# Moving GpSimd's work in a fused macaron block: low rows, paced preparation, a choice in three parts, attention's last copies

## The reference

```python
x = x + 0.5 * moe(ln(x))      # n=1  16 experts of 176, top 6, and a shared SwiGLU of 352
x = x + mamba(ln(x))          # n=2  selective scan, 512 channels, 16 states, length 256
x = x + 0.5 * moe(ln(x))      # n=3  the same weights as n=1
x = x + 0.5 * ffn(ln(x))      # n=4  SwiGLU of 1024 with Hadamard transforms
x = x + attention(ln(x))      # n=5  16 heads of 16, ALiBi, causal
x = x + 0.5 * ffn(ln(x))      # n=6  the same weights as n=4

# moe: scores = softmax(x @ gate_w.T); top 6, divided by their sum; out += c_e * (silu(g) * u) @ w2_e.T
# mamba: s = exp(d * A) * s + d * B * u ; y = sum_n(s * C_n) + D * u ; out = (y * silu(gate)) @ Wout.T
# ffn: x = fwht(x * SU_ug); up, gate; x = fwht(silu(gate) * up * SU_dp); down, times Wscale_dp
```

## Time and profile before

| | |
|---|---|
| median of 3 runs | 1979.33 us (1977.91 to 1980.43) |
| the profiled execution | 1978.87 us; its span, first to last instruction, 1976.9 us |
| busy TensorE, VectorE, ScalarE, GpSimd | 92%, 69%, 47%, 29% of the span |
| chain that ended last | TensorE 74%, VectorE 13%, issue 7%, ScalarE 6% |
| granted TensorE clock, mean | 0.978 of full speed |

### The profile page before, as it was taken

One profiled execution on the slowest core, in us unless ns is written; L12 is line 12 of the kernel. 1 busy time (PEld: TensorE's weight loads), 2 busy tenths in 40 slices (PEclk: granted clock), 3 DMA queues, 4 the chain that ended last, 5 costly groups with the idle time before them and its releaser, 6 DMA issues.

```text
span 1976.9 us, 26195 instructions
## 1 busy us (share of the span) xinstructions
PE 1827.5 (92%) x9417; PEld 1391.2 (70%) x9417; DVE 1368.7 (69%) x1867; ACT 935.9 (47%) x1776; POOL 577.7 (29%) x383
## 2 busy tenths in 40 slices
PE   7999899999797996998769999999999999998998
PEld 5788688888343543544327888888888887776887
DVE  6666756577999999989995566565676555666533
ACT  3442323333776766676533333232333338887322
POOL 1000604000487776876750000000000024555000
PEclk9999999999898998999999999999999998999999
DMA  5231244110221221221212132231221305552100
GB/s 189 78 105 62 88 150 118 65 61 25 65 69 57 67 70 52 66 65 63 104 44 84 39 104 80 86 102 65 65 73 52 62 1 130 113 111 64 35 11 22
DMA packets 84186, 146.39 MB, mean 74 GB/s; under 512 B 13848, under 2 KB 23704, under 8 KB 83544
## 3 DMA queue, kind: packets, MB, share of 16 engines
q1 hardware_dynamic: 84056, 144.72, 25.2%
HBM read 130.38 MB, written 14.29 MB: 73 GB/s over the span
## 4 chain that ended last, share of the span: by engine, by line
PE 74%; DVE 13%; issue 7%; ACT 6%; DMA 0%; POOL 0%; DVEq 0%; SPq 0%; ACTq 0%; POOLq 0%
PE psum L161 19%; PE psum L162 19%; PE psum L163 19%; DVE scan_state L1570 6%; PE psum L1390 5%; PE psum L1284 2%; PE psum L1944 1%; PE psum L1311 1%; DVE scan_state L1577 1%; PE psum L1370 1%; ACT psum L1497 1%; PE psum L1923 1%; DVE moe_hidden_lo L850 1%; PE psum L1961 1%; ACT attn_p L2092 1%
## 5 line engine op out<-in xcount | busy, mean ns | idle before, releaser
L1166 POOL TENSOR_TENSOR scan_state<-scan_delta_u,scan_B_rows 128x1024 f32<-128x1024 f32 x127 | 299.7, 2369 | 143.4 <-PE psum L1390 129.6
L161 PE MATMUL psum<-xnT_hi,moe_w_hi 128*128 128x512 f32 x800 | 317.9, 397 | 6.1 <-DVE xnT_lo L465 4.2
L162 PE MATMUL psum<-xnT_lo,moe_w_hi 128*128 128x512 f32 x800 | 315.4, 394 | 0.0
L163 PE MATMUL psum<-xnT_hi,moe_w_lo 128*128 128x512 f32 x800 | 313.0, 391 | 0.0
L1570 DVE TENSOR_TENSOR_SCAN scan_state<-psum,scan_state 128x1024 f32<-128x1024 f32 x128 | 292.2, 2283 | 2.3 <-ACT psum L1497 2.0
L777 ACT ACTIVATE moe_hidden<-psum 128x512 f32<-128x512 f32 x200 | 119.6, 598 | 367.5 <-PE psum L163 367.4
L827 DVE TENSOR_TENSOR moe_gated_up<-moe_gate_rows,psum 128x512 f32<-128x512 f32 x184 | 126.5, 688 | 211.4 <-PE psum L163 123.8
L1390 PE MATMUL psum<-scan_state,ident 128*128 128x512 f32 x512 | 255.8, 624 | 0.0
L161 PE MATMUL psum<-moe_w_hi,moe_hidden_hi 128*128 128x256 f32 x800 | 231.0, 289 | 15.9 <-DVE moe_hidden_lo L850 15.0
L413 POOL TENSOR_SCALAR rstd<-mean_var 128x2 f32<-128x2 f32 x48 | 10.5, 220 | 790.9 <-DVE mean_var L447 790.5
L163 PE MATMUL psum<-moe_w_hi,moe_hidden_lo 128*128 128x256 f32 x800 | 227.0, 284 | 0.0
(11 more groups left out here) (226 smaller groups left out, 3513.7 us busy)
## 6 DMA issues: line engine op xcount, KB each, us to landing
scan_B_rows<-scan_B SPq DMA_DIRECT2D x127, 256.0 KB, 3.1
moe_gate_rows<-gate_table SPq DMA_DIRECT2D x176, 128.0 KB, 2.9
...
```

The source lines that it names most:

```text
L161: e.matmul(out, wH, xH, start=start, stop=False)
L162: e.matmul(out, wH, xL, start=False, stop=False)
L163: return e.matmul(out, wL, xH, start=False, stop=stop)
L1166: e.tensor_tensor(self.st[q % self.NBUF][:], self.dtu[:, 2 * h:2 * h + 2, :], self.Bs[:, q % self.RING, :].unsqueeze(1).broadcast_to([P, 2 ...
```

## The change

1. **Scan's low rows.** `rows_lo` of chunks 1 to 3 goes from VectorE at r = 27 to GpSimd at r = 28, behind `times_u`, with a wait for `times_u` in front of it and a wait for itself behind it. That of chunk 0 stays on VectorE.
2. **Preparation in pieces.** The instructions on 1024 and 2048 elements per partition become pieces of 512, and each pair of pieces (or four scalings, or four taps) waits for one more `s_hL`: `Prep.pool` from step 41 to 50, `Scan.early` from step 60 to 67. SyncE's store of them comes at step 53, not 52.
3. **The choice in three parts and two banks.** In the entry, chunks 1 and 3 use bank 7 and chunks 0 and 2 bank 4, their logits, turns and gates come one step earlier (chunk 0's gates stay), and the choice is spread over three steps instead of two. In n=3 the choice has three parts too, and the gates follow one step later.
4. **Attention's last copies.** In the last two units ScalarE splits weight tile 0 before its copies, VectorE copies before it splits, and weight tile 2 of n=6 waits for the last product with V (`read`) instead of for all of attention's output (`freed`).

```diff
 # Tail.choose: part 0 up to the logits less their maximum, part 1 up to match_replace, part 2 the rest
-        k, n, t = self.k, [2 if part == 1 else 0], 4 * self.n
+        k, t = self.k, 4 * self.n
+        n = [(0, 2, 3 + 2 * t)[part or 0]]
...
+        if part == 1:
+            return
+        e.wait_ge(self.r_v.sem, self.r_v.at(3 + 2 * t, c))
         step(e.tensor_tensor(lg, ex, rest, ALU.subtract))
...
 # Glu
-    LATE = 52
-    PE_SLOTS = {2: 1, 3: 3, 5: 4, 6: 5, 9: 6}
-    ACT_SLOTS = {3: 1, 4: 3, 6: 4, 7: 5, 10: 6}
+    LATE = 53
+    PE_SLOTS = {2: 1, 3: 3, 5: 4, 6: 5, 10: 6}
+    ACT_SLOTS = {3: 1, 4: 3, 6: 4, 7: 5, 11: 6}
...
         if self.handed and n == 2:
-            self.prev.freed(e)
+            self.prev.read(e) if self.led else self.prev.freed(e)
...
 # Entry
-    LOGITS = {3: 0, 7: 1, 11: 2, 15: 3}
-    TURN = {4: 0, 8: 1, 12: 2, 16: 3}
-    GATES = {7: 0, 11: 1, 15: 2, 19: 3}
+    LOGITS = {3: 0, 6: 1, 10: 2, 14: 3}
+    TURN = {4: 0, 7: 1, 11: 2, 15: 3}
+    GATES = {7: 0, 10: 1, 14: 2, 18: 3}
...
+    def bank(self, c):
+        return self.k.psum[:, 7 if c % 2 else 4, :]
...
-            if self.LOGITS[j]:
-                e.wait_ge(t.r_cH.sem, t.r_cH.at(1, self.LOGITS[j] - 1))
-            t.pe(e, self.LOGITS[j], 4)
+            if c == 1:
+                e.wait_ge(t.s_xL.sem, t.s_xL.at(2, NCH - 1))
+            elif c:
+                e.wait_ge(t.r_cH.sem, t.r_cH.at(1, c - 2))
+            t.logits(e, c, self.bank(c))
...
 # Scan.early (PACE = 60)
-        e.tensor_copy(self.wH[:], self.raw[:]).then_inc(self.s_wh.sem, 1)
+        w, step = self.raw.shape[1] // 4, self.PACE
+        for n in range(4):
+            if n % 2 == 0:
+                e.wait_ge(self.prev.s_hL.sem, self.prev.s_hL.at(step + 1))
+                step += 1
+            e.tensor_copy(self.wH[:, n * w:(n + 1) * w], self.raw[:, n * w:(n + 1) * w]).then_inc(self.s_wh.sem, 1)
...
 # Scan.pool
+            if r == 28 and c + 1 < NCH:
+                e.wait_ge(self.s_dtu.sem, self.s_dtu.at(2 * c + 3))
+                self.rows_lo(e, c + 1)
+                e.wait_ge(self.s_bc.sem, self.s_bc.at(c + 2))
...
 # Scan.vector
-            if r == 27 and c + 1 < NCH:
-                rows_lo(c + 1)
...
 # Attention.scalar
+            if n == self.N - 2:
+                self.next.early_hi(e, 0)
+                keep(n, 0)
+                keep(n, 1)
             if n and n % 2 == 0:
                 out_hi(n // 2 - 1)
             job(c, u, 1)
-            keep(n, 0)
-            keep(n, 1)
-            if n + 2 >= self.N:
-                self.next.early_hi(e, n + 2 - self.N)
+            if n != self.N - 2:
+                keep(n, 0)
+                keep(n, 1)
+        self.next.early_hi(e, 1)
...
 # Prep.pool (PACE = 41), one of its three butterfly passes
-            e.tensor_tensor(b[:, :, 0, :], a[:, :, 0, :], a[:, :, 1, :], ALU.add).then_inc(self.s_d.sem, 1)
-            e.tensor_tensor(b[:, :, 1, :], a[:, :, 0, :], a[:, :, 1, :], ALU.subtract).then_inc(self.s_d.sem, 1)
+            for to, op in enumerate((ALU.add, ALU.subtract)):
+                e.wait_ge(self.moe.s_hL.sem, self.moe.s_hL.at(step + 1))
+                step += 1
+                for x in range(2):
+                    rows, cols = (slice(x * n, (x + 1) * n), slice(0, f)) if h < 4 else (slice(0, 1), slice(x * f, (x + 1) * f))
+                    e.tensor_tensor(b[:, rows, to, cols], a[:, rows, 0, cols], a[:, rows, 1, cols],
+                                    op).then_inc(self.s_d.sem, 1)
```

More of the change, by code:

```diff
@@ L363, in step @@
                 e.wait_ge(self.r_v.sem, self.r_v.at(n[0], c))
-        if part != 1:
+        if part in (None, 0):
             over = red.unsqueeze(2).broadcast_to([P, t, NEXP])
@@ L372, in choose @@
             return
-        e.wait_ge(self.r_v.sem, self.r_v.at(2, c))
-        e.wait_ge(self.r_ex.sem, self.r_ex.at(1, c))
-        for j in range(t):
-            if j == 0:
-                k.own(e)
-            step(e.max(mx[:, j, :], ex[:, j, :]), wait=(j == t - 1))
-        step(e.memset(mx[:, :, TOPK:8], -1.0))
-        for j in range(t):
-            if j == 0:
-                k.own(e)
-            step(e.match_replace(rest[:, j, :], mx[:, j, :], ex[:, j, :], 0.0), wait=(j == t - 1))
+        if part in (None, 1):
+            e.wait_ge(self.r_v.sem, self.r_v.at(2, c))
+            e.wait_ge(self.r_ex.sem, self.r_ex.at(1, c))
+            for j in range(t):
+                if j == 0:
+                    k.own(e)
+                step(e.max(mx[:, j, :], ex[:, j, :]), wait=(j == t - 1))
+            step(e.memset(mx[:, :, TOPK:8], -1.0))
+            for j in range(t):
+                if j == 0:
+                    k.own(e)
+                step(e.match_replace(rest[:, j, :], mx[:, j, :], ex[:, j, :], 0.0), wait=(part is None and j == t - 1))
+        if part == 1:
+            return
+        e.wait_ge(self.r_v.sem, self.r_v.at(3 + 2 * t, c))
         step(e.tensor_tensor(lg, ex, rest, ALU.subtract))
@@ L857, in vector @@
                 tail.low(e, tc, 1)
-            if tt in (7, 8) and self.guest:
+            if tt in (7, 8, 9) and self.guest:
                 tail.choose(e, tc, tail.bank(), tt - 7)
@@ L969, in dve_late @@
             t.stats(e, (j + 4) // 2, j % 2)
-        if j in self.TURN:
-            t.choose(e, self.TURN[j], self.k.psum[:, 4, :], 0)
-        if j - 1 in self.TURN:
-            t.choose(e, self.TURN[j - 1], self.k.psum[:, 4, :], 1)
+        for part in range(3):
+            if j - part in self.TURN:
+                c = self.TURN[j - part]
+                t.choose(e, c, self.bank(c), part)
         if j in self.BLOCKS:
@@ L1072 @@
     LOADS = 13
+    PACE = 60
     def u(self, c, i):
@@ L1141, in early @@
         e.wait_ge(self.s_load.sem, 16 * self.LOADS)
-        e.tensor_copy(self.wH[:], self.raw[:]).then_inc(self.s_wh.sem, 1)
-        e.wait_ge(self.s_wh.sem, self.s_wh.at(1))
-        e.tensor_tensor(self.wL[:], self.raw[:], self.wH[:].bitcast(F32), ALU.subtract).then_inc(self.s_wl.sem, 1)
+        w, step = self.raw.shape[1] // 4, self.PACE
[4 more added lines that the diff above has]
+            e.tensor_copy(self.wH[:, n * w:(n + 1) * w], self.raw[:, n * w:(n + 1) * w]).then_inc(self.s_wh.sem, 1)
+        e.wait_ge(self.s_wh.sem, self.s_wh.at(4))
+        for n in range(4):
+            if n % 2 == 0:
+                e.wait_ge(self.prev.s_hL.sem, self.prev.s_hL.at(step + 1))
+                step += 1
+            e.tensor_tensor(self.wL[:, n * w:(n + 1) * w], self.raw[:, n * w:(n + 1) * w],
+                            self.wH[:, n * w:(n + 1) * w].bitcast(F32), ALU.subtract).then_inc(self.s_wl.sem, 1)
         e.memset(self.mean[0][:], 1.0 / RANK).then_inc(self.s_one.sem, 1)
@@ L1221, in times_u, with rows_lo @@
         e.tensor_tensor(self.dtu[:, m, :], self.delta[:, m, :], self.pair(c, h), ALU.mult).then_inc(self.s_dtu.sem, 1)
+    def rows_lo(self, e, c):
+        e.wait_ge(self.s_bH.sem, self.s_bH.at(c + 1))
+        e.tensor_tensor(self.bc[32:32 + 2 * NST, c % 2, :], self.wt[1][:], self.bc[0:2 * NST, c % 2, :].bitcast(F32),
+                        ALU.subtract).then_inc(self.s_bc.sem, 1)
     def first_steps(self, e):
@@ L1546, in vector @@
         k, ps = self.k, self.k.psum
-        def rows_lo(c):
-            e.wait_ge(self.s_bH.sem, self.s_bH.at(c + 1))
-            e.tensor_tensor(self.bc[32:32 + 2 * NST, c % 2, :], self.wt[1][:], self.bc[0:2 * NST, c % 2, :].bitcast(F32),
-                            ALU.subtract).then_inc(self.s_bc.sem, 1)
         def convolve(i):
@@ L1614, in vector @@
         e.tensor_copy(self.bc[0:2 * NST, 0, :], self.wt[1][:]).then_inc(self.s_bH.sem, 1)
-        rows_lo(0)
+        self.rows_lo(e, 0)
         tail.both(e, NCH - 1, 1)
@@ L1739, in weight, with read @@
         return self.wH[:, at:at + HID], self.wL[:, at:at + HID]
+    def read(self, e):
+        e.wait_ge(self.s_pv.sem, self.s_pv.at(self.N))
     def freed(self, e):
@@ L2206, in vector @@
             job(c, u, 1)
-            if n + 2 >= self.N:
-                self.next.early_lo(e, n + 2 - self.N)
-        keep(self.N - 1)
+            if n == self.N - 2:
+                self.next.early_lo(e, 0)
+        self.next.early_lo(e, 1)
         out_lo(self.N // 2 - 1)
@@ L2234, in __init__ @@
         arena = Arena(k, "prep_")
-        arena.off = behind
+        arena.off = moe.end
         new = arena.new
```

50 lines of the change are left out of this document (31 added, 19 removed).

## The result

| | before | after |
|---|---|---|
| median of 4 runs | 1979.65 us (1977.91 to 1980.43) | 1929.9 us (1926.45 to 1931.35) |
| ratio, 95% interval | | 0.9747 [0.973, 0.9764] |
| the profiled execution, its span | 1978.87, 1976.9 us | 1931.35, 1929.4 us |
| busy TensorE, VectorE, ScalarE, GpSimd | 92%, 69%, 47%, 29% | 94%, 69%, 49%, 30% |
| granted TensorE clock, mean | 0.978 | 0.986 |

Faster by 50.1 us [46.7, 53.5]; 1935 with 1928 to 1947 had been forecast. I lay the two traces side by side by the start of each down(j). The lead of the changed kernel is then, in us: at down(39) 0.34, at down(44) 10.43, at down(56) 10.33, at down(61) 15.52, at the scan's start 15.52, at n=3's first down 37.79, at its end 38.3, at n=6's first down 46.13, at the end 47.5.

The account below looks back on a forecast made before the run. TensorE was taken to bound the expert and FFN stages, VectorE the scan, neither attention's end. Terms 14.6 + 20.6 + 7.8 + 1.3 = 44.3 us off 1978.87 gave 1934.6, forecast as a median of 1935, range 1928 to 1947.

Parts of the forecast that it names:

- What bounds the kernel: Whole kernel: TensorE bounds expert and FFN stages (4.19 us a step), VectorE the scan (3.50 a unit), neither attention's end.
- Part 2: n=1, down(39) to down(44) and down(56) to down(60): preparation in pieces ends VectorE's holds, saving 14.6 us.
- The 0.7 charged: n=1, steps 49 and 50: pieces start late after four scalings of 1.30 us and meet VectorE instructions, costing 0.7 us.
- Part 1: Scan: three low-row instructions, 22.95 us in all, leave VectorE, saving 20.6 us after charges.
- The 2.0 charged: Scan, chunks 1 and 2: the choice's subtraction now falls in GpSimd's run; 1.0 us charged for each.
- The margin of 0.4 us: Scan: GpSimd has chunk 1's first state ready at 633.4, VectorE reaches that unit at 633.85.
- Part 4: Attention's end to n=6's first down: reordered copies, earlier weight tile and regained half clock save 7.8 us.
- Part 3: Entry: logits of chunks 1 to 3 lose the bank wait, TensorE waits for gates instead; 1.3 us saved.
- A: n=1 preparation: pieces still collide, each of 12 pairs costs about 1.0 us, 12 us in all: 1946 us; chance 0.11.
- B: Scan, chunks 1 and 2: the choice's subtraction waits until GpSimd's run ends, 17 us: 1952 us; chance 0.06.
- C: Six steps beside scalings or taps: GpSimd's tensor_scalars block VectorE as well, 17 us: 1952 us; chance 0.02.
- D: n=1: VectorE holds GpSimd off, paced work, store and gate rows slip; slower, over 1979 us; chance 0.02.

## Why the prediction was right, point by point

**What bounds the kernel.** Right: where GpSimd no longer held VectorE, TensorE's stage ran at 4.2 us a step and the scan at VectorE's 3.50 a unit.

**Part 2, 14.6 forecast.** 10.1 + 5.2 = 15.3 in the trace, 15.2 [12.1, 18.6] alone. The lost time was read rightly. The 0.7 charged for pieces that come late was not needed: eight scalings took 8.21 us instead of 10.41, so four fit into a step. How much is lost differs from trace to trace: from down(39) to down(61) it was 107.3 to 110.8 us in eight traces that keep the stalls (108.1 in before), 92.9 in after.

**Part 1, 20.6 forecast.** 22.3 in the trace, 23.4 [20.8, 25.9] alone; right in mechanism, small by 1.7. The 2.0 charged for two choices were not needed: their subtraction took 0.54 and 0.97 us, but they had taken 0.63 and 0.79 in before already, so this cost 0.1. And TensorE's output job of chunk 3, for which VectorE had waited 1.79 us at unit 11, no longer came late, 1.69 us that I had not looked for. So the scan itself gave 23.7 us; 1.4 were lost again between its last unit and n=3's first down, which takes 22.4 to 24.4 us in the fourteen traces, with stretches of half clock at different places. The margin of 0.4 us for unit 32's state was 618.47 - 617.94 = 0.53.

**Part 4, 7.8 forecast.** From the transposes of P(30) on, gu(0) was to come 7.35 us later and did after 7.28; down(0) 14.65, and did after 14.61. The half clock gave back 1.41, not 1.0. That is 8.25. But this half clock does not always follow the idle stretch: in the nine traces that keep the 2.30 us idle, the step behind it takes 5.67 to 5.85 us in four and 4.26 to 4.28, the full-clock time, in five. The remaining 1.0 of the trace's 9.2 had come earlier in attention, where this change has nothing. It goes with the clock, though no run isolates it: the lead arises in attention's first four units, where both traces have stretches at half clock at different places. From n=4's last down to the transposes of P(30) the fourteen traces take 188.8 to 193.1 us, and before's is the longest.

**Part 3, 1.3 forecast.** 2.6 [0.4, 4.9] alone. In the trace of after the lead at down(39) is only 0.34 us. The first steps begin 0.54 later there, ahead of the choice; the entry gives 0.88, since step 4's half clock, some 1.6 us, falls into it; with the same clock it is 2.2 or more (above). Bank waits gave back 0.97 to 0.98 us a time instead of 0.76; TensorE's waits for the gates are 0.32, 0.64, 0.11 and 0.11 (up to 0.8, thrice, foreseen). In n=3, where nothing had been forecast, the new choice takes 420.0 us in four traces, the old one 420.16 to 420.55 in ten.

**The rivals.** A (pieces collide, 12 us): out, the paced pieces cost nothing; without the waits they cost 7. B (the choice is held instead): out, its subtraction took at most 0.97 us in the changed kernel and 2.22 in any of the fourteen traces. The mechanism is real, since L1550 was held 10.34 us, and the forecast had no reason but one case for why the choice would get in; that it did was in part luck. C (scalings and taps hold VectorE too): out, hidden and low part took 0.68 to 0.90 us beside them in all traces. D (slower): out, the last piece ended at 261.40 + 2.55 = 263.95, ahead of step 53.

The Trainium skill, "SBUF — State Buffer", section "Who interferes with whom", says of the ports that VectorE and GpSimd share that whoever issues first has them for the whole instruction; it says so of VectorE's two-port modes, and names instructions with two SBUF inputs beside them as contending. For the 128-partition instructions of n=1 that GpSimd's tensor_tensors held all runs agree (for example 4.83 us beside one of 4.60). For the 32 x 512 one they do not: 10.34 us over four instructions of 2.33 to 2.37; by that rule no hold would be over 2.4 us. The sum for part 1 took the 22.95 us from the rows, and they came back.

**The sum.** 44.3 forecast, 47.5 in the trace, 50.1 [46.7, 53.5] by the times. Taken alone, each part saved more than its term, but only part 1's term (20.6) lies outside its interval, by 0.2. A stall can cost not only its idle time but half clock behind it: part 2's lost time, read from the steps, held this already (3.3 of the 15.3), part 4's was put 0.4 too low. Since the half clock behind one and the same stall is there in some traces and not in others, a term read from one trace carries 1 to 2 us of chance at each such place. The forecast came within 3.2 us of the traces' difference, and part of what is left may be of this kind.
